# Adding v's bias to the attention rows of a transformer layer instead of to v itself

## The reference, cut to what matters

```python
kv = (_layernorm(x, kvn_g, kvn_b) @ Wkv + bkv).reshape(B, C, 2, H, hd)
k, v = kv[0], kv[1]                       # after a transpose
scores = einsum('bhqd,bhkd->bhqk', qn, kn) / sqrt(hd)   # causal mask
w = softmax(scores, axis=-1)
a = einsum('bhqk,bhkd->bhqd', w, v)
out = a.transpose(0, 2, 1, 3).reshape(B, C, Dm) @ Wo + bo
```

## Time and profile before

| what | value |
|---|---|
| median of 3 runs | 2143.21 us |
| profiled execution, its own time | 2141.41 us |
| its span (first to last instruction) | 2139.7 us |
| PE busy | 2083.7 us (97%) |
| DVE busy | 1568.8 us (73%) |
| ACT busy | 1106.2 us (52%) |
| POOL busy | 1277.4 us (60%) |
| mean granted TensorE clock | 0.982 |

### The profile page before, as it was taken

One profiled execution on the slowest core, in us unless ns is written; L12 is line 12 of the kernel. 1 busy time (PEld: TensorE's weight loads), 2 busy tenths in 40 slices (PEclk: granted clock), 3 DMA queues, 4 the chain that ended last, 5 costly groups with the idle time before them and its releaser, 6 DMA issues.

```text
span 2139.7 us, 41486 instructions
## 1 busy us (share of the span) xinstructions
PE 2083.7 (97%) x15432; PEld 1723.0 (81%) x15432; DVE 1568.8 (73%) x3545; ACT 1106.2 (52%) x2069; POOL 1277.4 (60%) x1285
## 2 busy tenths in 40 slices
PE   7999997899999999998999999999999999999998
PEld 4778886577777777775788889999999999999997
DVE  6788897787878878785892357777777677777765
ACT  4555552366666666665784434445444444544442
POOL 2667776234344343534327987777777777777773
PEclk9999998699999999999999999999999999999999
DMA  6323353656757667545988866565565656456553
GB/s 212 108 100 130 108 153 133 151 137 149 174 132 171 154 153 168 122 111 146 308 302 286 311 241 229 204 222 189 205 226 209 229 208 231 181 199 226 214 210 133
DMA packets 202977, 399.81 MB, mean 187 GB/s; under 512 B 24380, under 2 KB 107452, under 8 KB 202776
## 3 DMA queue, kind: packets, MB, share of 16 engines
q1 hardware_dynamic: 201112, 392.96, 57.6%
q10 hardware_dynamic: 1088, 3.15, 0.4%
q0 software_dynamic: 576, 1.07, 0.2%
HBM read 263.81 MB, written 82.33 MB: 162 GB/s over the span
## 4 chain that ended last, share of the span: by engine, by line
PE 77%; DVE 2%; ACT 1%; DMA 1%; issue 1%; POOL 0%; SPq 0%; ACTq 0%; DVEq 0%
PE b_psOL L1135 9%; PE f_psM L2082 9%; PE f_psM L2081 9%; PE f_psM L2080 9%; PE b_psB L1103 8%; PE b_psA L1076 6%; PE f_psD L2071 5%; PE f_psD L2070 5%; PE f_psD L2072 5%; PE b_psOL L1126 2%; PE b_psA L1063 2%; PE f_psM L2094 1%; PE f_psM L2096 1%; PE f_psM L2095 1%; PE f_psD L1526 1%
## 5 line engine op out<-in xcount | busy, mean ns | idle before, releaser
L1823 POOL TENSOR_TENSOR f_w_parts<-f_staged,f_w_parts 128x256 fp32r<-128x256 f32 x823 | 674.1, 854 | 222.0 <-ACT f_w_parts L1859 222.0
L1258 ACT ACTIVATE b_probT<-b_psB 128x512 f32<-128x512 f32 (+1 forms) x640 | 315.3, 556 | 138.2 <-PE b_psB L1103 138.2
L1174 DVE TENSOR_REDUCE b_top<-b_psA 128x2 f32<-128x1024 f32 (+2 forms) x320 | 284.4, 901 | 79.5 <-PE b_psA L1076 79.3
L2082 PE MATMUL f_psM<-f_h_odd,f_w_parts 128*128 128x256 f32 x896 | 253.6, 283 | 0.0
L2081 PE MATMUL f_psM<-f_h_odd,f_w_parts 128*128 128x256 f32 x896 | 253.0, 282 | 0.0
L2080 PE MATMUL f_psM<-f_h_odd,f_w_parts 128*128 128x256 f32 x896 | 253.0, 282 | 0.0
L1103 PEld LDWEIGHTS b_psB<-b_stack 98*128 98x128 f32 x1280 | 184.5, 190 | 74.3 <-issue 38.4
L1876 ACT ACTIVATE f_gu_hi<-f_gu 128x512 fp32r<-128x512 f32 x128 | 81.0, 633 | 307.9 <-DVE f_gu L1964 269.2
L1103 PE MATMUL b_psB<-b_stack 98*128 98x256 f32 (+1 forms) x1280 | 219.3, 291 | 7.4 <-ACT b_probT L1258 5.0
L1859 ACT ACTIVATE f_w_parts<-f_staged 128x768 fp32r<-128x768 f32 x237 | 210.8, 937 | 22.1 <-DMA f_staged<-parts_d 12.6
L2070 PE MATMUL f_psD<-f_wd_parts,f_gu_hi 128*128 128x512 f32 x512 | 201.5, 394 | 0.8 <-DMA f_wd_parts<-down_d 0.8
(11 more groups left out here) (223 smaller groups left out, 4913.3 us busy)
## 6 DMA issues: line engine op xcount, KB each, us to landing
f_staged<-parts_d SPq DMA_DIRECT2D x112, 896.0 KB, 5.6
f_wd_parts<-down_d SPq DMA_DIRECT2D x112, 512.0 KB, 3.7
b_stack<-b_halves SPq DMA_DIRECT2D x192, 256.0 KB, 4.8
qkv_d<-a_t SPq DMA_DIRECT2D x32, 512.0 KB, 2.7
b_land<-qkv_d SPq DMA_DIRECT2D x32, 512.0 KB, 4.9
parts_d<-f_staged SPq DMA_DIRECT2D x16, 896.0 KB, 4.4
a_x<-in_x SPq DMA_DIRECT2D x32, 256.0 KB, 3.5
qkv_d<-a_v SPq DMA_DIRECT2D x32, 256.0 KB, 3.2
```

Source lines behind the costliest of these rows:

```text
L1174: last = dve.tensor_reduce(into, tile[:, :, col:col + whole_blocks * P], AX.X, ALU.max, negate=True)
L1258: act.activation(probT[:, (NW * n + w) % PROBS, j, 0:width], psB[:, i % BANKS, 0:width], ACT.Exp).then_inc(s["expd"], 1)
L1823: op = pool.tensor_tensor(lo, whole, hi.bitcast(F32), ALU.subtract)
L2082: last = pe.matmul(out_n, hi[:, k], x_lo[:, k], start=False, stop=(k == 1))
```

## The change

The third bias matmul of each tile is gone: `product` and `first_product` add biases to q and k only, and v's last product closes its sum. The v part of the bias row (`brow`) is written once to DRAM and read back as one column of 128 per group of heads (`a.v_bias`, 128x4). `normalise` adds the column after its two multiplications, in two TENSOR_SCALAR of 128x512 behind a wait for them; `finish` adds it to each quarter. The counts of the semaphores `scaled`, `ended`, `mask_in` and `bias_in` follow.

```diff
@@ qkv_stage, SP, load(0, 3)
                     sp.dma_start(bias2[1:2 * HD + 2:HD, :].bitcast(F32), blo[0:2 * HD + 1:HD, :].bitcast(F32)).then_inc(bias_in, 16)
+                    sp.dma_start(scratch["v_bias"].ap(), brow[2 * HD:2 * HD + 1]).then_inc(bias_in, 16)
@@ SP, step 21
-                    a.load_consts(sp)
+                    sp.wait_ge(bias_in, 32)
+                    a.load_consts(nc, sp)
@@ DVE, first_unit
-                    dve.wait_ge(a.s["mask_in"], 16 * 9)
+                    dve.wait_ge(a.s["mask_in"], 16 * 10)
@@ PE, product
-                        pe.matmul(out, hT_lo[...], wqkv_hi[:, k, cols], start=False, stop=False)
-                    last = pe.matmul(out, chosen[:, m], bias2[:], start=False, stop=True)
+                        last = pe.matmul(out, hT_lo[...], wqkv_hi[:, k, cols], start=False, stop=(m == 2 and k == KC - 1))
+                    if m < 2:
+                        pe.matmul(out, chosen[:, m], bias2[:], start=False, stop=True)
@@ PE, first_product
-                pe.wait_ge(bias_in, 16)
-                for m in range(3):
+                pe.wait_ge(bias_in, 32)
+                for m in range(2):
@@ Attention.load_consts
+        with nc.allow_non_contiguous_dma(reason="a few columns"):
+            sp.dma_start(self.v_bias[:], self.scratch["v_bias"][0].rearrange("(g p) -> p g", p=P)).then_inc(self.s["mask_in"], 16)
@@ SP, store
-                    sp.wait_ge(s["scaled"], n + 1)
+                    sp.wait_ge(s["scaled"], 2 * n + 2)
-                    sp.wait_ge(s["ended"], NQ + 1)
+                    sp.wait_ge(s["ended"], 3 * NQ)
@@ POOL, normalise
+                if n == 0:
+                    pool.wait_ge(s["mask_in"], 16 * 10)
                 mul.then_inc(s["scaled"], 1)
+                pool.wait_ge(s["scaled"], 2 * n + 1)
+                for half in range(2):
+                    cols = slice(half * W, (half + 1) * W)
+                    add = pool.tensor_scalar(att[:, n % 2, cols], att[:, n % 2, cols], a.v_bias[:, n % GROUPS:n % GROUPS + 1], None, ALU.add)
+                add.then_inc(s["scaled"], 1)
@@ DVE, finish
-                dve.wait_ge(s["ended"], q + 1)
-                mul = dve.tensor_tensor(att[...], att[...], sums[...], ALU.mult)
-                if q == NQ - 1:
-                    mul.then_inc(s["ended"], 1)
+                dve.wait_ge(s["ended"], 3 * q + 1)
+                dve.tensor_tensor(att[...], att[...], sums[...], ALU.mult).then_inc(s["ended"], 1)
+                dve.wait_ge(s["ended"], 3 * q + 2)
+                dve.tensor_scalar(att[...], att[...], a.v_bias[:, n % GROUPS:n % GROUPS + 1], None, ALU.add).then_inc(s["ended"], 1)
@@ ACT, take
-                at_least(act, s["scaled"], n - 1)
+                at_least(act, s["scaled"], 2 * (n - 1))
```

More of the change, by code:

```diff
@@ L684, in product @@
                         pe.matmul(out, hi, wqkv_lo[:, k, cols], start=False, stop=False)
-                        pe.matmul(out, hT_lo[:, t % 2, k * P:(k + 1) * P], wqkv_hi[:, k, cols], start=False, stop=False)
-                    last = pe.matmul(out, chosen[:, m], bias2[:], start=False, stop=True)
+                        last = pe.matmul(out, hT_lo[:, t % 2, k * P:(k + 1) * P], wqkv_hi[:, k, cols], start=False, stop=(m == 2 and k == KC - 1))
+                    if m < 2:
+                        pe.matmul(out, chosen[:, m], bias2[:], start=False, stop=True)
                 last.then_inc(s["qkv_mm"], 1)
@@ L700, in first_product @@
                         pe.matmul(out, hi, wqkv_lo[:, k, cols], start=False, stop=False)
-                        pe.matmul(out, hT_lo[:, 0, k * P:(k + 1) * P], wqkv_hi[:, k, cols], start=False, stop=False)
-                pe.wait_ge(bias_in, 16)
-                for m in range(3):
+                        pe.matmul(out, hT_lo[:, 0, k * P:(k + 1) * P], wqkv_hi[:, k, cols], start=False, stop=(m == 2 and k == KC - 1))
+                pe.wait_ge(bias_in, 32)
+                for m in range(2):
                     last = pe.matmul(psQ[:, 0, m * DM:(m + 1) * DM], chosen[:, m], bias2[:], start=False, stop=True)
@@ L774, in __init__ @@
         self.ln_q = early("b_ln_q", [P, 2])
+        self.v_bias = early("b_v_bias", [P, GROUPS])
         self.top = early("b_top", [P, 2, 2, 4 * TB])
@@ L806, in rows_of, with load_consts @@
         return src[n // GROUPS]
-    def load_consts(self, sp):
+    def load_consts(self, nc, sp):
+        with nc.allow_non_contiguous_dma(reason="a few columns"):
+            sp.dma_start(self.v_bias[:], self.scratch["v_bias"][0].rearrange("(g p) -> p g", p=P)).then_inc(self.s["mask_in"], 16)
         for j in range(4):
@@ L1211, in finish @@
                 dve.reciprocal(sums[:, n % 2, cols], sums[:, n % 2, cols]).then_inc(s["ended"], 1)
-                dve.wait_ge(s["ended"], q + 1)
-                mul = dve.tensor_tensor(att[:, n % 2, cols], att[:, n % 2, cols], sums[:, n % 2, cols], ALU.mult)
-                if q == NQ - 1:
-                    mul.then_inc(s["ended"], 1)
+                dve.wait_ge(s["ended"], 3 * q + 1)
+                dve.tensor_tensor(att[:, n % 2, cols], att[:, n % 2, cols], sums[:, n % 2, cols], ALU.mult).then_inc(s["ended"], 1)
+                dve.wait_ge(s["ended"], 3 * q + 2)
+                dve.tensor_scalar(att[:, n % 2, cols], att[:, n % 2, cols], a.v_bias[:, n % GROUPS:n % GROUPS + 1], None, ALU.add).then_inc(s["ended"], 1)
             for k in STEPS:
@@ L2146, in layer @@
         "qkv": nc.dram_tensor("qkv_d", [NT, P, 3 * DM], F32),
+        "v_bias": nc.dram_tensor("v_bias_d", [1, DM], F32),
         "sums": nc.dram_tensor("sums_d", [2, 4, C], F32),
```

## The result

The changed kernel is slower: 2182.94 us (median of 4 runs, 2172.17 to 2190.56) against 2143.24 of the kernel before beside it, a ratio of 1.0177 [1.0159, 1.0196]. The forecast was 2140.9 us and its range ended at 2145.0. The profiled execution took 2188.92 us, its span is 2187.2 and its mean clock 0.969 (0.982 before).

The account below looks back on a forecast made before the run. PE was taken to bound the kernel, with a DVE-POOL loop nearly as long in the qkv stage. Terms -5.9 + 3.2 + 0.35 = -2.35 us took 2143.2 to 2140.9 us, range 2136.0 to 2145.0.

Parts of the forecast that it names:

- part 1: Qkv stage: 32 matmuls less save 7.5 us if PE alone sets the pace; 1.6 lost, gain 5.9 us.
- The loop through POOL: Qkv stage: a DVE, ACT and POOL loop of 9.45 us a step stands just behind PE's 9.56.
- a sign of being wrong: Qkv stage: shortening by 7 us or by less than 4 would show the forecast wrong.
- the rival in which DVE's loop sets every step: Qkv stage gains only 3.8 us, with the same POOL cost: 2143.0 us, no change; chance 0.11.
- a loss of about 0.2: Qkv stage: the step at 116.60 already starts on `a_hn` and loses its 0.23 us.
- Part 2: Attention: POOL's adds lengthen `normalise` by 1.4 us, delaying the cut and costing PE 3.2 us.
- The bound from above: `normalise`: at the two-input rate of L1040 the adds and their wait take at most 2.8 us.
- The place and the spares: Cut behind `normalise`: in 13 places PE loses the delay plus 0.05 us less the spare, wherever positive.
- The kernel is slower: Rival at the cut behind `normalise`: delay of 2.8 us costs 19.5 us, giving 2157 us; chance 0.17.
- Part 3 and 4: Last unit: DVE's add in `finish` costs 0.35 us; bias row store and column load are hidden, costing nothing.
- POOL's adds deciding: Rival at the cut behind `normalise`: delay beyond the spares is paid 13 times, kernel slower; chance 0.17.

Follow-up runs that it names:

- the broadcast: Changed kernel with POOL's adds as two-input operations, the bias column broadcast, in the old place; 2154.95 us, ratio 1.0050.
- the half: Changed kernel with only the first of the two adds of each `normalise`, the upper half of the columns without bias; 2145.47 us, ratio 1.0006.
- run 12: Changed kernel with its one-operation adds, in an edit meant to issue them behind the cut that left them in front; 2177.05 us, ratio 1.0156.
- run 3: Changed kernel with the constant 0.0 in place of the bias column in POOL's adds; 2172.54 us, ratio 1.0133.
- run 8: Changed kernel, complete, with SP issuing the loads of the inverted sums in step 7 instead of 8; 2153.89 us, ratio 1.0047.
- run 5: Changed kernel with all adds in the cheap form: column added and multiplied by 1.0 in one instruction; 2143.03 us, ratio 0.9996.
- run 14: Changed kernel with its one-operation adds issued behind the cut, in the second step, instead of in front; 2171.16 us, ratio 1.0126.

## Why the prediction was wrong

- **What bounds the kernel, and part 1: the mechanism right, the gain too high by the traces.** The loop through POOL held as forecast: steps of 9.45 us behind 283, 9.31 in the quiet stretch, L409 growing by 0.12 us a step. The gain was 5.9 by forecast; the trace of the change has 4.0 at the first scores (3.98, just under the 4 that the prediction named as a sign of being wrong, and close to the 3.8 of the rival in which DVE's loop sets every step, which the steps of 9.31 us rule out), the run without adds 6.5 by medians and 4.3 by profiled spans. Two losses were sized too low: the first transposes came 0.57 us later (54.15 against 53.58), and the step at 283.37 began with 1.20 us of waiting, where a loss of about 0.2 was forecast.
- **Part 2: the step that failed.** Its sentence was "four single-input operations of this size take 2.37 us, so two take 1.2". The adds take 3.1 to 3.2 us a unit, and PE's waits for the cut come to 24.4 us in the 13 places where the sum had 3.2. The row was a true one, of another form: L1795 is written with two operations (1.0, 1.0, both multiplications), and the add with one. The profile prints both as TENSOR_SCALAR; the difference is in the code alone. The bound from above failed too: "the two-input rate", 2.8 us, is no ceiling for a one-input operation. By the estimate from the Trainium skill (GPSIMD Engine Reference, section 3.1, Elementwise), 0.44 us for a body of at most two operations, the one-operation form should be no dearer than the two; the rows have 1.49 against 0.62, so the measurement decides against it.
- **The place and the spares: right in sum, not place by place.** The prediction's own sum with the measured delay is 13 x (3.2 + 0.05) - 17.5 = 24.8 us, and the 13 pieces have 24.4. At the cheap form's delay of 1.45 us it gives 3.6, measured 4.0; at the broadcast's 2.0 it gives 9.3, measured 10.5; at the half's 1.7 it gives 5.9, measured 4.1. The single pieces agree less: in the sixth place the spare of 2.22 leaves 1.03 us, and 2.19 were measured, in the seventh 2.01 and 1.01. So part of the agreement of the sums may be luck.
- **The price of a wait: missing from every rival.** "The kernel is slower" ended at 2157 for 19.5 us of waits, each us counted once. With this much waiting for the cut the clock of the stretch falls as well. By the profiled spans a us of added waiting cost 2.2 us in the kernel after (51.8 for 23.9), 1.7 in run 12 (40.6 for 24.3) and 1.5 in run 3 (30.0 for 19.8), but 1.1 in run 8, where the clock stayed up until 950 us (16.8 for 15.3). Run 3, with about the waits of that rival, took 2172.5.
- **Part 3 and 4: nothing against them.** DVE's add is there with 0.35 us (1004.68 in run 5), and no wait for the constants shows at DVE's step. In the chain of work that ended last, the load behind the last multiplication starts at 1005.49 in run 5 and at 1005.12 in the kernel before, with the multiplication at 1004.22 and 1004.23: 0.38 us for part 3's 0.35, in one execution of each.
- **The chances.** POOL's adds deciding had 0.17 with its condition written out: "a column operand was never seen on POOL". The doubt was put on the operand; it belonged to the form of the instruction.

## What to carry to other kernels

A duration may be taken over from another row only if the instruction is the same in the code too: number of operations, operands, types. On POOL try a lone add or multiplication by a scalar also with a second, neutral operation, and time both forms. Where PE has no idle time, list the spare of each thing that queues behind an addition; once the delay is past the spares, count the stall and then look at the clock behind it. An engine's idle share is no room: POOL, ACT and DVE each had some, and each placement made another queue late.

## What the runs showed of the hardware

- GpSimd's TENSOR_SCALAR on 128x512 f32: 1.49 us with one operation and a constant, 1.57 (median) with one and a column, 0.62 with two constants, 0.69 with a column and a constant; TENSOR_TENSOR with a broadcast column 1.07, with two full inputs 1.31.
- A DVE operation with two inputs of 32 columns takes 0.19 us alone and 1.22 beside POOL's two-input operations, until those end.
- The holding goes both ways. In run 14 DVE's low part (128x1024, two inputs) starts at 597.53, 0.08 us behind POOL's cut, and takes 2.10 us, the cut 1.10; in the run without adds it starts at 591.57, 0.03 us ahead of the cut, and takes 1.22, the cut 2.14.
